# Order of the weight setup in a fused decoder layer: folded weights and K of chunk 0 ahead of the head weights, with other unread products between them

## The reference, cut to what matters

```
q_in = x @ Wq.T + bq
Q3   = conv1d(q_in, convq_w, convq_b, 3 taps)
Q    = [q_in, Q3] @ qproj_w.T + qproj_b          # the same for K with Wk, convk, kproj
tau   = sigmoid(conv1x1(gelu(depthwise conv3(x, tau1)), tau2))     # 16 heads
delta = sigmoid(conv1x1(gelu(depthwise conv3(x, del1)), del2))
scores = (Q . K) / sqrt(8) * tau + delta
x = layernorm(x + softmax(scores) @ V @ out_w.T + out_b)
x = layernorm(x + mLSTM cross attention(x, context))
x = layernorm(x + FP6-quantised linear(x))
```

## Time and profile before

| | us |
|---|---|
| median of 3 runs | 213.35 (212.99 to 213.43) |
| the profiled execution | 213.28 |
| its span, first to last instruction | 211.3 |

### The profile page before, as it was taken

One profiled execution on the slowest core, in us unless ns is written; L12 is line 12 of the kernel. 1 busy time (PEld: TensorE's weight loads), 2 busy tenths in 40 slices (PEclk: granted clock), 3 DMA queues, 4 the chain that ended last, 5 costly groups with the idle time before them and its releaser, 6 DMA issues. The chain is left out here.

```text
span 211.3 us, 6086 instructions
## 1 busy us (share of the span) xinstructions
PE 193.3 (91%) x2103; PEld 122.0 (58%) x2103; DVE 159.6 (76%) x432; ACT 140.8 (67%) x427; POOL 102.4 (48%) x218
## 2 busy tenths in 40 slices
...
PEclk9965599999999999999999999999999999999999
...
DMA packets 12137, 9.38 MB, mean 44 GB/s; under 512 B 2796, under 2 KB 10828, under 8 KB 12108
## 3 DMA queue, kind: packets, MB, share of 16 engines
...
q10 hardware_dynamic: 992, 0.04, 0.3%
...
## 5 line engine op out<-in xcount | busy, mean ns | idle before, releaser
L1129 DVE TENSOR_REDUCE nm<-score 128x8 f32<-128x1024 f32 x32 | 38.8, 1218 | 6.9 <-PE score L662 6.8
L520 ACT ACTIVATE prob<-score 128x1024 f32<-128x1024 f32 x32 | 32.5, 1020 | 11.1 <-PE score L674 11.0
L662 PE MATMUL score<-km,qf 32*128 32x512 f32 x128 | 33.9, 637 | 1.2 <-DVE nm L1129 0.3
L668 PE MATMUL score<-qm,kf 32*128 32x512 f32 x128 | 33.8, 636 | 0.0
L388 POOL CAST nmx<-nm 128x16 bf16<-128x16 f32 x16 | 5.5, 341 | 31.2 <-issue 26.2
L674 PEld LDWEIGHTS score<-nmT,sel 32*128 32x128 bf16 x256 | 10.1, 93 | 16.2 <-issue 16.2
L359 POOL TENSOR_SCALAR u<-xTp,dw 128x512 f32<-128x512 f32 x16 | 13.7, 868 | 10.3 <-PE score L740 5.4
L883 PE MATMUL bankPV<-prob,vw 128*32 128x128 f32 x512 | 17.2, 275 | 0.0
L583 ACT ACTIVATE dec<-dec,g 128x128 f32<-128x128 f32 x56 | 17.1, 393 | 0.0
L656 PE MATMUL bankP<-xTp,wT 128*128 128x512 f32 x36 | 16.8, 602 | 0.0
L422 POOL TENSOR_TENSOR hsl<-hs,rows 128x256 f32<-128x256 f32 (+1 forms) x9 | 6.0, 672 | 20.4 <-ACT hs L599 20.4
(11 more groups left out here) (264 smaller groups left out, 491.1 us busy)
## 6 DMA issues: line engine op xcount, KB each, us to landing
...
```

What stands on the lines that cost most here:

```text
L520: nc.scalar.activation(prob[:, i % 2, k:k + 2, :].rearrange("p k s -> p (k s)"), sc[:, 512 * k:512 * (k + 2)], ACT.Exp, scale=SQ_SCALE).th ...
L662: ins = mm(sc[:, 512 * k:512 * (k + 1)], qf[r, n, :], km[r, n % (2 * CB)].rearrange("p j s -> p (j s)"), start=True, stop=True)
L668: mm(sc[:, 512 * k:512 * (k + 1)], kf[r, n, :], qm[r, n % (2 * CB)].rearrange("p j s -> p (j s)"), start=True, stop=False)
L1129: nc.vector.tensor_reduce(nm[:, i % 3, J * k:J * (k + 2)], sc[:, 512 * k:512 * (k + 2)].rearrange("p (h s) -> p h s", s=S), AX_X, ALU.max, ...
```

## The change

Three tables of steps or lines change; no instruction's shape does.

- PE: mT.1 comes directly behind tx.1. wT.0, tx.2 and wT.1 follow, with 5, 2, 1 and 3 unread products ahead of or behind them, then K.0, and only then hw.0, cT.0, Q.0, tau.0 and del.0. Before, hw.0 stood ahead of mT.1, and cT.0, del.0 and tau.0 ahead of K.0.
- DVE: both mT evictions come ahead of tapD.0 and tapT.1; wT.1 and bias.0 come ahead of tapD.2, and hw.0 and wd.0 behind it. The order from tapT.2 on is the same.
- The `light` products (12 before, 23 now) are written to score bank S3 instead of PV.
- Late in PE's list `fill.2 fill.5` becomes `fill.7`, and there is a new `fill.1` between hst.6 and hT.6 and a new `fill.2` between hst.8 and hT.8.

ACT, POOL and SP keep their lists. The core of the diff:

```diff
-    light.8 tx.0 light.1 ab.0 light.3 mT.0 tx.1 hw.0 mT.1 wT.0 tx.2 wT.1 cT.0 del.0 tau.0 K.0 Q.0 gw.0 tx.3 K.1 cg.0 aa.0 fill.2 tau.1 fill.2 cT.1 fill.1
...
-    qk.5 pT.8 MT.6 ffn.3 yT.7 fill.2 fill.5 gF.7 aT.8 hst.5 qk.6 hT.5 ld.7 dT.4 y1.8 MT.7 qk.7 ffn.4 yT.8 fill.2 hst.6 hT.6 fill.2 gF.8 hst.7 qk.8 fill.2 MT.8
...
+    light.8 tx.0 light.1 ab.0 light.3 mT.0 tx.1 mT.1 light.5 wT.0 light.2 tx.2 light.1 wT.1 light.3 K.0 hw.0 cT.0 Q.0 tau.0 del.0 gw.0 tx.3 K.1 cg.0
...
-    fil.0 cent.0 sel.0 ab.0 tapT.0 tapD.0 mT.0 tapT.1 hw.0 mT.1 tapD.1 wT.0 tapD.2 wd.0 bias.0 wT.1 tapT.2 kf.0 bias.1 tapT.3 qf.0 gw.0 qs.0 tapD.3 kf.1
...
+    fil.0 cent.0 sel.0 ab.0 tapT.0 mT.0 mT.1 tapD.0 tapT.1 wT.0 tapD.1 wT.1 bias.0 tapD.2 hw.0 wd.0 tapT.2 kf.0 bias.1 tapT.3 qf.0 gw.0 qs.0 tapD.3
...
-                        mm(pvb[:], fil[:], fil[:].unsqueeze(1).to_broadcast([P, NH, S]), start=True, stop=True)
+                        mm(sc[:, 1536:2048], fil[:], fil[:].unsqueeze(1).to_broadcast([P, NH, S]), start=True, stop=True)
```

More of the change, by code:

```diff
@@ L55 @@
 PE_ORDER = """
-    light.8 tx.0 light.1 ab.0 light.3 mT.0 tx.1 hw.0 mT.1 wT.0 tx.2 wT.1 cT.0 del.0 tau.0 K.0 Q.0 gw.0 tx.3 K.1 cg.0 aa.0 fill.2 tau.1 fill.2 cT.1 fill.1
-    aa.1 nmT.0 Q.1 v1.2 nmT.1 fill.5 v1.3 edT.0 V.0 ow.0 fill.1 v2.2 V.1 rc.0 fill.2 v2.3 del.1 pv.0 nmT.2 K.2 v1.4 edT.1 pv.1 V.2 v2.4 pT.0 nmT.3 cm.0
-    v1.5 aT.0 nmT.4 cm.1 y1.0 v2.5 yT.0 pv.2 del.2 pv.3 gF.0 v1.6 MT.0 tau.2 pT.1 del.3 nmT.5 aT.1 tau.3 y1.1 Q.2 v2.6 Q.3 qk.0 edT.2 pv.4 edT.3 cT.2
-    hst.0 nmT.6 v1.7 cT.3 hT.0 gF.1 cm.2 v2.7 K.3 v1.8 nmT.7 pv.5 V.3 MT.1 v1.9 yT.1 pT.2 V.4 v2.8 aT.2 cm.3 dT.0 y1.2 qk.1 pv.6 ffn.0 v2.9 nmT.8 hst.1
@@ L64 @@
-    ld.8 hT.7 dT.5 fill.2 ffn.5 fill.5 hst.8 hT.8 dT.6 fill.2 ffn.6 fill.8 dT.7 fill.2 ffn.7 fill.9 dT.8 fill.2 ffn.8
+    light.8 tx.0 light.1 ab.0 light.3 mT.0 tx.1 mT.1 light.5 wT.0 light.2 tx.2 light.1 wT.1 light.3 K.0 hw.0 cT.0 Q.0 tau.0 del.0 gw.0 tx.3 K.1 cg.0
+    aa.0 fill.2 tau.1 fill.2 cT.1 fill.1 aa.1 nmT.0 Q.1 v1.2 nmT.1 fill.5 v1.3 edT.0 V.0 ow.0 fill.1 v2.2 V.1 rc.0 fill.2 v2.3 del.1 pv.0 nmT.2 K.2
+    v1.4 edT.1 pv.1 V.2 v2.4 pT.0 nmT.3 cm.0 v1.5 aT.0 nmT.4 cm.1 y1.0 v2.5 yT.0 pv.2 del.2 pv.3 gF.0 v1.6 MT.0 tau.2 pT.1 del.3 nmT.5 aT.1 tau.3 y1.1
@@ new lines @@
+    Q.2 v2.6 Q.3 qk.0 edT.2 pv.4 edT.3 cT.2 hst.0 nmT.6 v1.7 cT.3 hT.0 gF.1 cm.2 v2.7 K.3 v1.8 nmT.7 pv.5 V.3 MT.1 v1.9 yT.1 pT.2 V.4 v2.8 aT.2 cm.3
+    dT.0 y1.2 qk.1 pv.6 ffn.0 v2.9 nmT.8 hst.1 cm.4 yT.2 v1.10 hT.1 pv.7 nmT.9 v2.10 pT.3 gF.2 v1.11 aT.3 MT.2 V.5 nmT.10 y1.3 v2.11 yT.3 pv.8 v1.12
+    V.6 pv.9 qk.2 nmT.11 cm.5 pT.4 v2.12 hst.2 gF.3 V.7 hT.2 aT.4 dT.1 v1.13 ffn.1 nmT.12 pv.10 v2.13 y1.4 V.8 MT.3 pv.11 v1.14 pT.5 nmT.13 cm.6 v2.14
+    aT.5 gF.4 v1.15 y1.5 MT.4 cm.7 qk.3 nmT.14 pv.12 yT.4 v2.15 hst.3 dT.2 cm.8 pv.13 hT.3 yT.5 bb.14 nmT.15 pT.6 gF.5 ffn.2 aT.6 qk.4 y1.6 pv.14 yT.6
```

28 lines of the change are left out of this document (14 added, 14 removed).

## The result

| | before | after |
|---|---|---|
| median of 20 executions each, us | 213.39 (212.89 to 214.21) | 211.22 (210.00 to 213.84) |
| ratio, with its 95% interval | | 0.9895 (0.9873 to 0.9917) |
| the profiled execution, us | 213.28 | 212.26 |
| its span, us | 211.3 | 210.3 |
| its mean granted clock | 0.966 | 0.977 |

The account below looks back on a forecast made before the run. TensorE was taken as the bound, its weight setup at half clock for 13.5 us, with nmT.0's start passed on to the end. 0 at the tail plus 2.3 us gained, off 213.28, gave 211.0; range 209.9 to 213.1.

Parts of the forecast that it names:

- The clock at the start, and TensorE's steps: Weight setup on TensorE: clock stays up, K.0 starts at 16.8 us instead of about 25.8, tau.0 ends at 26.8.
- DVE's wait for the head weights: DVE at the hw.0 evictions: reaches them at 20.7 us and waits until 21.8.
- 2.3 us earlier, by POOL and not by DVE: POOL's queue behind tau.0: split.0 starts at 37.75 us instead of 40.06; DVE's mX.0 would be 3.1 earlier.
- R5: Rival: POOL is faster than taken and DVE sets the gain, 3.1 us or a little more, 210.0; chance 0.04.
- Who interferes with whom: POOL products beside DVE taps: by this rule each waits out a whole tap, and the gain would be 1.5 us.
- R1: Rival: clock dips behind the head weights' new place, costing 1.1 to 1.7 us of the gain, 212.3; chance 0.13.
- the prediction's own sign of being wrong: TensorE's start: the forecast is wrong if the clock level falls anywhere ahead of tau.0.
- R2: Rival: clock dips while TensorE waits 2 us for nmT.0, 2 us less gain, 213.0; chance 0.06.
- delays nobody: aa.0 on TensorE: runs at 33.2 us instead of 35.45, holding nothing up since mX.0 is due at 34.5.
- R3: Rival, slower: unread products don't hold the level, it falls at 12.6 us as before, 215.5; chance 0.13.
- R4: Rival: no effect, or POOL's queue and then TensorE's waits among the softmax steps take back 2.3 us, 213.2; chance 0.04.
- The tail: End of TensorE's list: new fill.1 and fill.2 fit in waits ahead of hT.6 and hT.8, costing 0.

Follow-up runs that it names:

- run 11: Changed kernel plus fill.2 ahead of y1.8 and fill.1 ahead of qk.7 in the tail; median 210.65 us, ratio 0.9872.
- run 6: Changed kernel with POOL's km.0 and tapD.3 ahead of tapT.4 and tapT.5, which wait for tau.0; median 211.54 us, ratio 0.9891.
- run 12: The changed kernel as it is, timed once more; median 211.77 us, ratio 0.9893.
- run 1: Changed kernel without the eleven new unread products around wT.0, tx.2 and wT.1; median 215.6 us, ratio 1.0008 resting on five of twelve executions.
- run 5: Changed kernel with eight more unread products between cg.0 and aa.0 on PE; median 210.87 us, ratio 0.9886.
- run 8: Changed kernel with tau.0 ahead of Q.0 and two more unread products between cT.0 and tau.0; median 212.47 us, ratio 0.9947.
- run 3: Changed kernel with DVE's tapD.0 again ahead of both mT evictions; median 216.76 us, ratio 1.0045 resting on five of twelve executions.
- run 4: Changed kernel with hw.0 again ahead of mT.1 on PE and its evictions early on DVE; median 212.22 us, ratio 0.9940.
- run 7: Changed kernel without the new fill.1 ahead of hT.6 and fill.2 ahead of hT.8; median 212.47 us, ratio 0.9910.
- run 2: Kernel before, in its old order, plus the eleven unread products, written to bank S3; median 211.52 us, ratio 0.9882.
- run 9: Changed kernel with POOL's km.0 and tapD.3 first, three unread products behind hw.0, and fills ahead of y1.8 and qk.7; median 210.42 us, ratio 0.9854.
- run 10: Kernel before, old order, plus the eleven unread products, the change's fill.1 and fill.2, and fills ahead of y1.8 and qk.7; median 209.69 us, ratio 0.9825.

## Why the prediction was right, and where not

**The clock at the start, and TensorE's steps: right.** The level stays up through the setup, to 33.2 in the profiled execution. wT.0 at 11.52 (11.5 said), wT took 1.56 (1.7), K.0 at 16.26 (16.8), tau.0 ended at 26.05 (26.8), aa.0 started at 33.13 (33.2), nmT.0 at 39.69 (39.8). No step up to nmT.0 is off by over 0.75 us. The span that no row of before showed at the upper level, wT with its narrow products, came out near the lower bound of 1.5.

**DVE's wait for the head weights: wrong, harmless.** 1.1 us was said, from 20.7 to 21.8; DVE came later, at 21.42, and found them done, as PE had gone on to the next step at 21.10.

**"2.3 us earlier, by POOL and not by DVE": right size, wrong cause.** POOL's terms were mis-sized, but for the single product (1.12): the three products took 2.46 (3.0 said), km.0 4.21 (3.13), qm.0 2.70 (3.56). The sum is 10.5 where 10.8 was said, with a start 0.56 earlier, so qm.0 ended at 36.66, 1.0 before the forecast. In the profiled execution split.0 then waited 1.02 us for DVE. What delayed DVE was aa.0 at the lower level: mX.0 waited 1.17 for it. Undisturbed (run 11) both engines end together, qm.0 at 33.95 + 2.69 = 36.64 and DVE's maxima at 34.29 + 2.36 = 36.65. There mX.0 still waits 0.28 for aa.0, and so for POOL's km.0; run 6 takes this wait away, but DVE's step ahead of mX.0 then starts 0.34 later (33.68 instead of 33.34), and the best time is the same. That is case R5, priced at 210.0 with a chance of 0.04; four of the first 20 executions and one of the six of run 12 are it, at 210.0 to 210.2. The 2.39 of the profiled execution is the 3.29 of run 11 less 0.90 for the fall at aa.0, so that it meets the forecast of 2.3 is luck.

The Trainium skill, SBUF — State Buffer, section "Who interferes with whom", weighed in the prediction, would have each product of POOL wait out a whole tap of DVE. The rows agree in direction: four POOL instructions take 2.69 beside DVE's maxima, which read only a score bank, and its waits, and 4.21 beside its taps and scaling (28.68 to 32.9), whichever step stands there (in run 6 it is POOL's products, and km.0 takes 3.13). They do not show a wait of a whole tap for each product: three products took 2.46 in the new place and 2.03 in the old. The price belongs to the place and not to the step; the prediction carried km.0's price of before to a new place.

**The rivals.** R1 (behind the head weights) was seen in runs 1, 5, 8 and 12 at 21 to 25 us, and in run 3 at 25.6, behind head weights that ran later. Its price on tau.0, 1.7, is right: tau.0 started at 25.88 instead of 24.17 in run 5. The 1.1 to 1.7 said for the whole is right too: nmT.0 came at 40.04 in run 12 and at 38.79 in run 11, 1.25 apart. It is no case beside the forecast, but something that some executions have: a fall ahead of tau.0 was the prediction's own sign of being wrong, and the changed kernel's second profile (run 12) shows it where the first does not. R2 named the wait ahead of nmT.0; the fall came one wait earlier, at aa.0, behind idleness of the length that the text gives (about 2 us), and cost 0.9. Of the five profiles with a wait of 1.7 us or more there four fall within 1.4 us of aa.0's start (the changed kernel, runs 1, 4 and 7) and one doesn't (run 11); of those with 1.44 or less none does. That the wait brings it about is likely by that, not shown. The prediction had computed that aa.0 "delays nobody" and did not ask what its own wait does to the clock. The 2 us of waiting that it named stood at aa.0 (1.91); at nmT.0 it was 0.22, and 0.75 in run 11. R3 (slower, 215.5) is near what run 1 is without the new products (median 215.6), but in its one profile the level fell at other places than 12.6. R4 did not happen among the softmax steps.

**The tail: not foreseen.** The rows of before show the upper level there, and the sum took 0. The fall at 183 cost 1.36 in the profiled execution. It needed no new idleness: the waits ahead of it (0.54 and 0.30) are short, between products with 32 rows or 16 small ones in a row. It is in the profiles of after and of runs 1, 3, 6, 8 and 12, and not in those of before and of runs 2, 4, 5 and 7. With fills in front of those steps three profiles of three are free of it (runs 9, 10, 11), and run 10, which differs from run 2 in the tail alone (and was timed on another chip), has clocks of 0.988 to 0.990 in all five executions, where run 2 has 0.975 to 0.989 in six, four of them at 0.983 or less. None of the 16 executions of runs 9 to 11 has a clock below 0.985; of the 26 of the changed kernel 12 have 0.983 or less. That the fills do it is likely by that, not certain.

**What stands for the median.** The forecast was worked out for an execution without a fall and a slow POOL. The measured median, 211.2, is a middle of executions without a fall (210.0), with a short one (about 211: run 7's profile has one of 3.4 us and took 210.66) and with more or longer ones (212.3 to 213.8; run 6's has one of 6.8 us and took 212.10). That the two agree so closely is partly luck.

**What the change rests on.** The prediction gave the gain to the whole change. Runs 1 and 2 show that the eleven unread products bring it (0.9882 by themselves against 1.0008 for the rest, or 0.992 against 1.011 by the medians of all executions), and runs 10 and 11 that the old order does at least as well with them: kf.0 starts at 25.4 and 25.1 us. With tau.0 early POOL starts sooner, and a fall at 12 or 13 us is nearly hidden.

**Open.** Why one execution of the same program falls behind the head weights, another at aa.0, another not at all, was not settled: run 11 and the profiled execution of the change have the same wait of 1.91 us at 31.2 to 33.1, and only one falls. One row does go with the fall behind the head weights. TensorE's first transposes, tx.0 at 4.5 us, stand just ahead of or at the first rise of the level; here those of run 5 and of the changed kernel:

```profile
4.42 0.63 PE L684 MATMUL score<-ident,xt 128*128 128x128 f32 x4
```

```profile
4.51 1.06 PE L685 MATMUL score<-ident,xt 128*128 128x128 f32 x4
```

In the five profiles with that fall (runs 1, 3, 5, 8 and 12) they took 0.63 to 0.91, so the level was up early; in the five without it that have the head weights in the new place (the changed kernel, runs 6, 7, 9 and 11) 1.06 to 1.09, so it rose later. Where the first rise lies differs between executions of the same program (0.74 in run 12, 1.06 in the first profile of the changed kernel), and the fall seems to go with it. Ten profiles show that the two go together, not what sets them. Where the fall lies in the three slower executions of run 11 isn't known, since the profiled one is one of those without.
